# Row maxima of 14-wide attention: brought into the scores by a product instead of by row transfers

## The reference, cut to what matters

```
x = pad(x)                      # 16 x 16 to 28 x 28, then 4 windows of 14 x 14 per image
attn = einsum('bqc,bkc->bqk', q * scale, k)
attn = attn + rel_h[..., None] + rel_w[..., None, :]     # from q and the position tables
attn = softmax(attn, axis=-1)   # over the 196 keys of a window
out = attn @ v
```

## Time and profile before

| | |
|---|---|
| median of 3 runs | 658.7 us (655.34, 658.7, 663.69) |
| span of the profiled execution | 663.8 us |
| TensorE busy | 581.6 us (88%) |
| VectorE busy | 299.0 us (45%) |
| ScalarE busy | 221.1 us (33%) |
| GpSimd busy | 154.6 us (23%) |
| mean granted TensorE clock | 0.906 |

### The profile page before, as it was taken

One profiled execution on the slowest core, in us unless ns is written; L12 is line 12 of the kernel. 1 busy time (PEld: TensorE's weight loads), 2 busy tenths in 40 slices (PEclk: granted clock), 3 DMA queues, 4 the chain that ended last, 5 costly groups with the idle time before them and its releaser, 6 DMA issues.

```text
span 663.8 us, 9874 instructions
## 1 busy us (share of the span) xinstructions
PE 581.6 (88%) x3696; PEld 425.6 (64%) x3696; DVE 299.0 (45%) x824; ACT 221.1 (33%) x437; POOL 154.6 (23%) x239
## 2 busy tenths in 40 slices
PE   7977875799999989899997998989878886999997
PEld 5737663573766667576675694766567655755777
DVE  3756673552132353435555443135576655610133
ACT  4214452524143025234342415143144445242020
POOL 7004221203004044053352207001041222030021
PEclk9997676887998999899999899998985877999999
DMA  6981545004313426625545305400924530020001
GB/s 163 211 185 28 136 87 149 2 1 110 76 40 85 90 73 139 140 74 109 131 101 119 96 1 124 100 18 27 191 51 95 110 85 3 1 61 0 1 0 48
DMA packets 22956, 54.14 MB, mean 82 GB/s; under 512 B 5842, under 2 KB 11578, under 8 KB 22814
## 3 DMA queue, kind: packets, MB, share of 16 engines
q1 hardware_dynamic: 20990, 53.20, 34.1%
q0 software_dynamic: 1920, 0.32, 0.4%
HBM read 10.94 MB, written 0.79 MB: 18 GB/s over the span
## 4 chain that ended last, share of the span: by engine, by line
PE 65%; DVE 11%; DMA 9%; SPq 7%; issue 3%; ACT 2%; POOL 2%; DVEq 0%; POOLq 0%; ACTq 0%
PE PS L1171 63%; DMA QA<-NR 6%; DVE NM L1067 4%; DMA QA<-REL 2%; SPq L704 2%; PE PS L1187 2%; SPq L696 1%; SPq L714 1%; DMA PT<-in_qm 1%; SPq L653 1%; ACT REL L902 1%; DVE HL L1080 1%; DVE OT L1104 1%; POOL KHL L796 1%; DVE OT L1102 1%
## 5 line engine op out<-in xcount | busy, mean ns | idle before, releaser
L1067 DVE TENSOR_REDUCE NM<-PS 98x2 f32<-98x392 f32 (+2 forms) x192 | 105.4, 569 | 98.8 <-PE PS L1171 97.0
L1171 PE MATMUL PS<-QA,KA 128*98 128x196 f32 (+2 forms) x480 | 103.0, 331 | 28.1 <-DMA QA<-NR 24.5
L922 ACT ACTIVATE PT<-PS 98x392 f32<-98x392 f32 (+2 forms) x192 | 94.3, 520 | 94.5 <-PE PS L1171 90.3
L1171 PE MATMUL PS<-KA,QA 126*98 126x196 f32 (+3 forms) x432 | 100.9, 333 | 15.0 <-DVE NM L1067 12.1
L1171 PEld LDWEIGHTS PS<-QA,KA 128*98 128x98 f32 (+2 forms) x480 | 80.3, 218 | 41.5 <-DMA QA<-NR 27.6
L1171 PEld LDWEIGHTS PS<-KA,QA 126*98 126x98 f32 (+3 forms) x432 | 68.7, 203 | 41.0 <-DVE NM L1067 21.2
L818 POOL DMA_DIRECT2D QA<-NR x60 | 35.0, 585 | 214.8 <-DVE NR L1091 214.8
L1171 PE MATMUL PS<-XT,W 96*128 96x512 f32 x144 | 66.6, 618 | 3.4 <-issue 3.4
L1171 PE MATMUL PS<-XT,WQKV 96*96 96x512 f32 x128 | 62.9, 623 | 5.3 <-issue 4.1
L1171 PE MATMUL PS<-PT,V 128*32 128x196 f32 (+2 forms) x672 | 58.1, 400 | 0.0
L1171 PE MATMUL PS<-W,HT 128*128 128x192 f32 x288 | 48.7, 328 | 4.7 <-ACT HT L943 4.7
(11 more groups left out here) (97 smaller groups left out, 667.7 us busy)
## 6 DMA issues: line engine op xcount, KB each, us to landing
QA<-QHL SPq DMA_DIRECT2D x36, 192.0 KB
KA<-KHL SPq DMA_DIRECT2D x24, 228.0 KB
QA<-REL SPq DMA_DIRECT2D x24, 224.0 KB
QA<-QHL SPq DMA_DIRECT2D x12, 384.0 KB
KA<-KHL SPq DMA_DIRECT2D x12, 384.0 KB
KA<-PT SPq DMA_DIRECT2D x12, 380.0 KB
W<-in_w SPq DMA_DIRECT2D x6, 576.0 KB, 5.8
QA<-REL SPq DMA_DIRECT2D x24, 128.0 KB
```

What stands on the lines that cost most here:

```text
L922: nc.scalar.activation(dst, src, ACT.Exp).then_inc(probs_done.sem, 1)
L1067: nc.vector.tensor_reduce(dst, src, AX.X, ALU.max, negate=True).then_inc(max_done.sem, 1)
L1171: return nc.tensor.matmul(dst, lhsT, rhs, start=start, stop=stop, skip_group_check=loose)
```

## The change

In the 14-wide layers the negated maxima no longer lie in `QA`. Rows 126 and 127 become two more rows of masks (zeros). `HL` keeps high and low part of the ten columns in two halves, so that VectorE writes each by one instruction. TensorE turns the even and the odd columns by one transposition each into the two halves of a row of PSUM (10 x 240), VectorE copies it to `NR`, which now has 128 rows, of which 118 stay zero. Each unit of scores gets one product more, added onto the two that are there: a selector `SEL` (128 x 5, two ones in a column; an input `HOT`, copied once by ScalarE) with one column spread over all keys as weights, and `NR` as what is streamed, its columns repeated for both halves of the unit. GpSimd's transfers for these layers go. The maxima run two heads in front instead of three.

```diff
-        self.max_row = 126
+        self.max_row = 128 if self.pads else 126
...
-    later, ahead = chunk_units(1), 3
+    later, ahead = chunk_units(1), 2
     for j in range(ahead * L.max_units):
         out.append(("max", j // L.max_units, j % L.max_units, 0))
-        if j % 4 == 0 and j < 16:
-            out.append((*later[j // 4], 2 + j // 4 % 2))
-        if j % L.max_units == 1 and j > L.max_units:
-            m = j // L.max_units - 1
-            out += [("maxT", m, 0, 0), ("aug", 4 + m, 0, 0)]
+        if j % 3 == 0:
+            out.append((*later[j // 3], 2 + j // 3 % 2))
+        if j == L.max_units + 1:
+            out += [("maxT", 0, 0, 0), ("aug", 4, 0, 0), ("aug", 5, 0, 0)]
...
-        goal = min(len(maxima), h * L.max_units + 2 if h else 3)
+        goal = min(len(maxima), h * L.max_units + 5)
...
-        for dst, src in ((EPS[:, :], io["eps"]), (COL[0][:, :], io["col0"])):
+        for dst, src in ((EPS[:, :], io["eps"]), (COL[0][:, :], io["col0"]), (HOT[:, :], io["hot"])):
...
+            if L.pads:
+                nc.gpsimd.memset(m["NM"][:, :, :], 0.0)
+                nc.gpsimd.memset(m["NR"][:, :, :].bitcast(F32), 0.0).then_inc(hl_zero.sem, 1)
...
-            elif step == "maxT":
+            elif step == "maxT" and not L.pads:
                 pool.wait_ge(*maxT_done.at(n, h))
-                if L.pads:
-                    moves = [(row[:, 0:FIRST_EDGE], m["NR"][0:4 * NB, p, 0:HALF_IN]),
-                             (row[:, FIRST_EDGE:], m["NR"][4 * NB:, p, :])]
...
-        act.wait_ge(*first_in.at(0, 1))
+        act.wait_ge(*first_in.at(0, 2))
+        nc.scalar.activation(SEL[:, :], HOT[:, :], ACT.Copy).then_inc(sel_done.sem, 1)
         nc.scalar.activation(WARM[:, :], EPS[:, :], ACT.Sqrt)
...
+                    half = half_cols(L)
+                    hi, lo = m["HL"][:, p, 0:half], m["HL"][:, p, half:]
+                    nc.vector.tensor_copy(hi, nm).then_inc(max_hi.sem, 1)
+                    nc.vector.tensor_tensor(lo, nm, hi.bitcast(F32), ALU.subtract).then_inc(max_lo.sem, 1)
...
             elif step == "maxT":
-                    dve.wait_ge(*max_row_at(L, h - 2))
+                    dve.wait_ge(*(scores_psum.at(n, L.units * (h - 1) - 1) if L.pads else max_row_at(L, h - 2)))
+                if L.pads:
+                    dst, src = m["NR"][0:half_cols(L), h % 2, :], PS[0:half_cols(L), TR_BANK, 0:2 * L.max_rows]
...
+                if L.pads:
+                    for part in range(2):
+                        last = nc.tensor.transpose(PS[0:half_cols(L), TR_BANK, part * rows:(part + 1) * rows],
+                                                   hl[:, part::2], IDN[0:rows, 0:rows])
...
             elif step == "scores":
-                if k == 0:
+                if k == 0 and not L.pads:
                     pe.wait_ge(*max_row_at(L, h))
...
-                                  m["QA"][0:L.rows, 0, s, inner_keys(k)], True, True)
+                                  m["QA"][0:L.rows, 0, s, inner_keys(k)], part == 0, False, True)
...
+                if L.pads:
+                    if k == 0:
+                        pe.wait_ge(*maxT_done.at(n, h))
+                    rows = m["NR"][:, h % 2, :]
+                    size = HALF_IN if k < NB else EDGES if k == NB else L.pc
+                    if k < NB:
+                        rows = rows.rearrange("r (p q) -> r p q", p=2)[:, :, 0:HALF_IN]
+                    if k != NB:
+                        rows = rows.unsqueeze(1).broadcast_to([128, 2, *rows.shape[1:]])
+                    wide = 2 * INNER if k < NB else (2 if k == NB else 4) * EDGES
+                    last = mm(PS[0:size, bank, 0:wide], SEL[:, min(k, NB)].unsqueeze(1).broadcast_to([128, size]),
+                              rows, False, True, True)
```

More of the change, by code:

```diff
@@ L117, in key_constants @@
     masks = np.zeros((L.max_row - L.mask_row, n), np.float32)
-    ones = np.ones((2, n), np.float32)
+    ones = np.ones((L.rows - L.max_row, n), np.float32)
     def place(j, kh, kw):
@@ L501, in _build @@
     idn_in = count("idn_in", [1, 0, 0, 0], 16)
-    first_in = count("first_in", [2, 0, 0, 0], 16)
+    first_in = count("first_in", [3, 0, 0, 0], 16)
+    sel_done = count("sel_done", [1, 0, 0, 0])
     const_in = count("const_in", [3, 4, 4, 0], 16)
@@ L539, in _build @@
     maxT_done = count("maxT_done", [HEADS] * 3 + [0])
-    max_row_in = [count(f"max_row_in{p}", per(lambda L: HALF * L.max_dmas), 16)
+    max_row_in = [count(f"max_row_in{p}", per(lambda L: 0 if L.pads else HALF), 16)
                   for p in (0, 1)]
@@ L575, in max_row_at, with half_cols @@
     def max_row_at(L, h):
-        return max_row_in[h % 2].at(L.index, (h // 2 + 1) * L.max_dmas - 1)
+        return max_row_in[h % 2].at(L.index, h // 2)
+    def half_cols(L):
+        return L.max_cols // 2
     def chunk_read(L, c):
@@ L811, in _ @@
                 pool.wait_ge(*maxT_done.at(n, h))
-                if L.pads:
-                    moves = [(row[:, 0:FIRST_EDGE], m["NR"][0:4 * NB, p, 0:HALF_IN]),
-                             (row[:, FIRST_EDGE:], m["NR"][4 * NB:, p, :])]
[L815 to L818, removed]
+                nc.gpsimd.dma_start(raw(row), raw(m["NR"][:, p, :])).then_inc(max_row_in[p].sem, 16)
             elif step == "divide":
@@ L1057, in _ @@
                 h, p, j = i, i % 2, L.max_units * i + u
+                if L.pads and j == 0:
+                    dve.wait_ge(*hl_zero.at(n, 0))
                 dve.wait_ge(*max_psum.at(n, j))
@@ L1263, in _ @@
                 claim(TR_BANK, maxT_done.at(n, h))
-                nc.tensor.transpose(PS[0:L.max_cols, TR_BANK, 0:L.max_rows], m["HL"][:, h % 2, :].bitcast(F32),
-                                    IDN[0:L.max_rows, 0:L.max_rows]).then_inc(maxT_psum.sem, 1)
+                hl, rows = m["HL"][:, h % 2, :].bitcast(F32), L.max_rows
+                if L.pads:
+                    for part in range(2):
+                        last = nc.tensor.transpose(PS[0:half_cols(L), TR_BANK, part * rows:(part + 1) * rows],
+                                                   hl[:, part::2], IDN[0:rows, 0:rows])
+                else:
+                    last = nc.tensor.transpose(PS[0:L.max_cols, TR_BANK, 0:rows], hl, IDN[0:rows, 0:rows])
+                last.then_inc(maxT_psum.sem, 1)
             elif step == "scores":
                 h, k, s = i, u, i % L.ring
-                if k == 0:
+                if k == 0 and not L.pads:
                     pe.wait_ge(*max_row_at(L, h))
@@ L1289, in _ @@
                                   m["KA"][0:L.rows, 0, s, edge_keys(e)],
-                                  m["QA"][0:L.rows, 0, s, edge_queries(e)], True, True)
+                                  m["QA"][0:L.rows, 0, s, edge_queries(e)], e == 0, False, True)
                 else:
@@ L1294, in _ @@
                                   m["KA"][0:L.rows, 0, s, pad_keys_of(pc)],
-                                  m["QA"][0:L.rows, 0, s, FIRST_EDGE:NT], True, True)
+                                  m["QA"][0:L.rows, 0, s, FIRST_EDGE:NT], pc == 0, False, True)
+                if L.pads:
+                    if h + k == 0:
+                        pe.wait_ge(*sel_done.at(0, 0))
+                    if k == 0:
[9 more added lines that the diff above has]
+                              rows, False, True, True)
                 last.then_inc(scores_psum.sem, 1)
@@ L1461, in _pack @@
     arrays["qm"] = query_masks()
+    arrays["hot"] = np.zeros((128, NB + 1), np.float32)
+    for b in range(NB + 1):
+        arrays["hot"][b::NB + 1, b][:2] = 1
     arrays["idn"] = np.eye(128, dtype=np.float32)
```

25 lines of the change are left out of this document (9 added, 16 removed).

## The result

The changed kernel takes **644.4 us** (median of four runs, 635.57 to 644.92) against 659.55 us of the kernel before in the same comparison: a ratio of 0.972, interval 0.964 to 0.980, so faster. Forecast were 645 us, range 631 to 669. The profiled execution took 643.97 us with a span of 642.2 against 663.8; its mean granted clock is 0.957 instead of 0.906.

What follows compares the result with a forecast made beforehand. The head loops were taken as bound by TensorE, its clock and the transfers it waits for. Loops -11.8 and starts -2.5 summed to -14.3 us: 645 us against the median of 658.7, range 631 to 669.

Steps and rivals of the forecast that it cites:

- Waits for rows, -20.7 us: Head loops of layers 0 and 2: TensorE's waits for the row transfers, 12.2 + 8.5 us, go.
- under the name NR, as the rival had it: Head loops: the new products wait for NR behind VectorE, 0.5 us per head, 12 us back: 657 us; chance 0.05.
- "late next" in head 1: Head 1: VectorE's 2.9 us query splitting loses its cover; 1 us of it left as delay, head 8.2 us.
- The product, 1.25 us per head at full clock: Every head: new products cost between 1.05 and 1.52 us at full clock, taken as 1.25; 1.93 at half.
- A quarter at half clock: Head loops: a quarter of the time at half clock, giving 76.2 us a loop, 152.4 for both against 164.2.
- not over 90: Head loops: a sign of being right was TensorE busy over 90 per cent of them.
- Ahead of the loops, -2.5 us: Before the first scores: maxima move into the loops; 2.5 us less for both layers, between 4.4 less and 1 more.
- The sum: Whole kernel: -11.8 for the loops and -2.5 ahead of them, -14.3 us.
- The step that failed: Head loops: products cost 30 to 46 us, more than the waits removed, so only a better clock can pay.
- has half as many columns again between the same waits: Head loops: reason given for less half clock, more TensorE columns per head; a quarter of the time at half clock.
- the gaps are what goes: Head loops: clock rises follow gapless feeding, so removing gaps raises the clock; argued against the clock staying as now.
- The rival of the slow clock: Every head: products with 118 zero rows may not earn clock; 673 to 686 us; chance 0.13, including products twice as dear.

Runs made afterwards that it cites:

- experiment 4: Changed kernel with the selector loaded on GpSimd's queue and copied by ScalarE behind the first layer-norm: 641.1 us, ratio 0.970 to the kernel before.
- Experiment 1: Kernel before, row transfers and old order kept, plus one product of zeros over 128 rows per unit of scores: 656.0 us, ratio 0.993.
- Experiment 7: Changed kernel in the old order of the maxima, without the new products (neither row transfers nor product): 638.4 us, ratio 0.978 to the kernel before.
- experiment 5: Changed kernel with the new product given ten rows instead of 128: 756.6 us, ratio 1.148 to the kernel before.
- experiments 5 and 9: Changed kernel with the new product given ten rows (experiment 5) or 64 rows (the other): the 64-row run took 723.5 us, ratio 1.095 to the kernel before.
- experiment 10: Changed kernel with the product over ten rows and a product of zeros over 128 rows ahead of it in every unit: 749.8 us, ratio 1.134.

## Why the prediction came out right, and where its reason was wrong

- **Waits for rows, -20.7 us**: they went, and not under the name NR, as the rival had it. But half of that came back under another name: 8.7 and 8.6 us of waits for NM stand in the loops; I had counted 3.4 for heads 5 and 9, 1 for head 1 and 1.2 for head 10. The splitting of queries, "late next" in head 1, is part of it: head 1 takes 9.8 us from its first exponential to that of head 2, where I had 8.2.
- **The product, 1.25 us per head at full clock**: 1.11, inside the bounds and nearer to the unbroken row, since a pair of 196 columns too takes 0.18 in this stream and not 0.26. For the same reason a plain head is done in 3.70 us of TensorE and not in 4.5. From first exponential to first exponential heads 6 and 7 of layer 0 still take 4.4 and 4.5: head 6 is in part at half clock (0.79), and behind head 7 the first step of products with the values, 0.80, comes before the next exponential. Heads 4 and 8 take 9.3 (forecast 9.1), heads 5 and 9 6.3 (6.2). The loops came out at 76.6 and 74.9 (76.2) with errors against each other: cheaper products, more waits, less half clock. That the sum is so close is in part luck. One price was misread: a position unit at its modelled length of 1.34, where the row behind it says 1.16 from start to start (485.76 to 486.92):

```profile
486.92 0.40 PE L1171 MATMUL PS<-KA,QA 126*98 126x196 f32 x2
```
- **A quarter at half clock**: 18 and 10 per cent. TensorE is busy 86 per cent of the loops, not over 90.
- **Ahead of the loops, -2.5 us**: +1.8 in layer 0 and -4.0 in layer 2, -2.2 together. The +1.8 holds the second table load and the clock of the first 25 us (experiment 4).
- **The sum**: -13.9 us from loops and starts in the profiled runs, -14.3 forecast. The profiles themselves differ by 21.6: the rest lies in code that the change doesn't touch, 3.8 of it in layer 1 with 6.8 us at half clock there instead of 13.7. The medians differ by 15.2; the profiled run of before lay 5.1 us above its median.
- **The step that failed is the cause of the clock.** I wrote that only a better clock can make the change pay, and gave two reasons for the clock: a head "has half as many columns again between the same waits", and "the gaps are what goes". The theory that I took into the experiments was the second. Experiment 1 keeps half of the waits for rows, with TensorE idle for 30.4 us, and has the clock. Experiment 7 takes the transfers away without the products and gains 25 us in the loops, while the clock rises by 0.06 and 0.08 only. So it is mostly the added columns that bring the clock, the first reason; the gain is that of the waits, and of the product's 27 us only 6 to 7 are left to pay. I had priced the product as work added at a given clock, and had not asked what it does to the clock where the waits stay.
- **The rival of the slow clock** ("118 rows are zero and do not count") fell the other way round: products of nothing but zeros bring the clock (experiment 1), and leaving the zero rows out loses it and 112 us (experiment 5). The rule that I cited from the Trainium skill ("TensorE: Matmul & The Clock Gate", "Why this matters for your kernels") says of a single product over 32 rows that it takes as long as one over 128. No run here shows a single one. With 128 rows of which 118 are zero the product took 0.33 us at half clock, as the pair of scores before it; with ten rows given, between neighbours of 128, a unit took 1.48 us at half clock and 0.98 with 128.

Not settled: whether the holes at a change of shape or the missing rows keep the clock at 0.50, once it is there, in experiments 5 and 9; experiment 10 was meant to tell and shows both levels. And why products of zeros raise the clock is seen, not explained.

## What to carry to other kernels

Where TensorE's clock is low in a loop with waits, price added TensorE work net, by an experiment that adds it and removes nothing: here 27 us of products cost 6 to 7 us in the loops, or less than nothing, by what else stood there. Try a small product padded to the shape of its neighbours before cutting it to what it needs: here the cut cost 79 us (64 rows) and 112 (ten). Once transfers no longer set the pace, look for the next late engine in the waits: moving three units of maxima out of each of four heads to where VectorE has time gave 6.4 us by the medians, over a third of what the whole change had given.

## What the runs showed of the hardware that was not expected

- A product over 64 or ten rows between products over 128 rows costs 0.50 us more per unit at half clock (1.48 against 0.98), the same for 64 and ten; neither its weight load nor the next one is ahead of its product. Between 126 and 128 rows nothing of the kind is seen: in experiment 1 at full clock the steps between them take 0.18 to 0.19 us.
- A TensorE that the profile calls busy for the whole of a window (17.60 of 17.60 us) stayed at 0.50 (experiment 5): "busy" in the profile can include such holes.
- The same heads by the same code ran at 0.50 in one layer and at 1.00 in the other (experiment 10).
- Products of nothing but zeros over 128 rows raised the clock of the loops from 0.73 and 0.71 to 0.88 and 0.91, with half of the waits for rows still there (experiment 1).
